# Self-attention with a hand-written step order: one transpose, two loads and one ScalarE pair change their places

## The reference

```
h = _layernorm(x, ln1_g, ln1_b)
x = x + _mha(h, h, sa_wq, sa_bq, sa_wk, sa_bk, sa_wv, sa_bv, sa_wo, sa_bo)
...
scores = jnp.einsum('bhqd,bhkd->bhqk', q, k) * HD ** (-0.5)     # 16 heads of 32 channels
p = jax.nn.softmax(scores, axis=-1)
o = jnp.einsum('bhqk,bhkd->bhqd', p, v)
return o @ wo.T + bo
```

## Time and profile before

| | us |
|---|---|
| median of 3 runs (3400.57 to 3406.2) | 3404.1 |
| the profiled execution | 3406.2 |
| its span | 3404.4 |
| PE busy in it | 3162.3 (93%) |
| DVE, ACT, POOL busy | 1820.2 (53%), 1574.4 (46%), 1327.8 (39%) |
| mean granted clock of PE | 0.964 |

### The profile page before, as it was taken

One profiled execution on the slowest core, in us unless ns is written; L12 is line 12 of the kernel. 1 busy time (PEld: TensorE's weight loads), 2 busy tenths in 40 slices (PEclk: granted clock), 3 DMA queues, 4 the chain that ended last, 5 costly groups with the idle time before them and its releaser, 6 DMA issues. The chain is left out here.

```text
span 3404.4 us, 41927 instructions
## 1 busy us (share of the span) xinstructions
PE 3162.3 (93%) x14480; PEld 2509.9 (74%) x14480; DVE 1820.2 (53%) x2848; ACT 1574.4 (46%) x2980; POOL 1327.8 (39%) x1355
## 2 busy tenths in 40 slices
PE   6599997999999976999999999849999799999999
PEld 5478876888888864677777777537787588888887
DVE  4588863333223224888788888758887432222221
ACT  2366653322222213777777777716666232222222
POOL 0344541333333331766666666734554111111110
PEclk8799998999999997999999999979999899999999
DMA  3423313211111114344444434332231321111000
GB/s 132 124 57 89 87 54 115 84 50 50 44 47 47 41 44 121 105 123 108 109 124 122 115 97 110 95 103 60 82 84 54 114 78 38 38 38 38 32 28 27
DMA packets 215045, 264.33 MB, mean 78 GB/s; under 512 B 78459, under 2 KB 100579, under 8 KB 214835
## 3 DMA queue, kind: packets, MB, share of 16 engines
q1 hardware_dynamic: 214835, 261.66, 26.0%
HBM read 125.12 MB, written 60.42 MB: 55 GB/s over the span
## 5 line engine op out<-in xcount | busy, mean ns | idle before, releaser
L1101 DVE TENSOR_REDUCE L1sa_nmax<-L1sa_s 128x2 f32<-128x1024 f32 x256 | 310.5, 1213 | 135.1 <-PE L1sa_s L907 134.2
L1206 POOL TENSOR_TENSOR L1sa_El<-L1sa_E,L1sa_Eh 128x1024 fp32r<-128x1024 f32 x128 | 314.0, 2453 | 129.2 <-ACT L1sa_Eh L1000 124.5
L468 DVE TENSOR_TENSOR L1ff_gl<-L1ff_gf,L1ff_gh 128x512 fp32r<-128x512 f32 x128 | 94.4, 738 | 474.7 <-ACT L1ff_gh L428 474.7
L468 DVE TENSOR_TENSOR L0ff_gl<-L0ff_gf,L0ff_gh 128x512 fp32r<-128x512 f32 x128 | 98.4, 769 | 437.9 <-ACT L0ff_gh L428 437.9
L414 ACT ACTIVATE L1ff_gf<-L1ff_f,cols 128x512 f32<-128x512 f32 x128 | 88.3, 690 | 450.3 <-PE L1ff_f L94 450.3
L414 ACT ACTIVATE L0ff_gf<-L0ff_f,cols 128x512 f32<-128x512 f32 x128 | 88.3, 690 | 449.8 <-PE L0ff_f L94 449.8
L1009 ACT ACTIVATE L1sa_E<-L1sa_st 128x1024 f32<-128x1024 f32 x256 | 258.9, 1011 | 8.6 <-PE L1sa_st L919 8.6
L92 PE MATMUL L1ff_f<-L1ff_hTh,L1ff_Wh 128*128 128x512 f32 x512 | 203.1, 397 | 5.7 <-POOL L1ff_hTl L235 5.7
L92 PE MATMUL L0ff_f<-L0ff_hTh,L0ff_Wh 128*128 128x512 f32 x512 | 202.9, 396 | 5.7 <-POOL L0ff_hTl L235 5.7
L1000 ACT ACTIVATE L1sa_Eh<-L1sa_E 128x1024 fp32r<-128x1024 f32 x192 | 200.6, 1045 | 0.2
L93 PE MATMUL L1ff_f<-L1ff_hTh,L1ff_Wl 128*128 128x512 f32 x512 | 200.3, 391 | 0.0
(11 more groups left out here) (282 smaller groups left out, 8531.4 us busy)
## 6 DMA issues: line engine op xcount, KB each, us to landing
L1sa_OLN<-L1sa_osb SPq DMA_DIRECT2D x128, 192.0 KB, 2.7
L0ff_xs<-x SPq DMA_DIRECT2D x64, 256.0 KB, 2.9
L1sa_stack_q<-L1sa_parts_q SPq DMA_DIRECT2D x128, 128.0 KB, 2.6
L1sa_stack_k<-L1sa_parts_k SPq DMA_DIRECT2D x128, 128.0 KB, 2.6
L1ff_xs<-x SPq DMA_DIRECT2D x64, 256.0 KB, 3.5
L0ca_xs<-in_x SPq DMA_DIRECT2D x32, 256.0 KB, 3.1
L0ca_stage<-in_x SPq DMA_DIRECT2D x32, 256.0 KB, 2.8
x<-L0ca_stage SPq DMA_DIRECT2D x32, 256.0 KB, 2.0
```

The source lines that it names most:

```text
L468: nc.vector.tensor_tensor(gl[:, j % 2, :], gf[:, j % 2, :], f32(gh[:, j % 2, :]), ALU.subtract)\
L1101: nc.vector.reduce_max(nmax[:, h % 2, 2 * (n % 2):2 * (n % 2) + 2], s_bank[:, :, :], AX.X, negate=True)\
L1206: nc.gpsimd.tensor_tensor(El[:, n % 2, :], E[:, n % 3, :], f32(Eh[:, n % 2, :]), ALU.subtract)\
```

## The change

Three edits, all in the order of the self-attention stage.

1. `SA_T_HALVES`: tile 1 of the next image is transposed in half 26 (step 13), not in half 24 (step 12).
2. On SP the load of tile 3 of the next image moves from step 13 to step 14, and the load of tile 1 of the image after that from step 16 to step 17.
3. On ACT the pair `o_hi` of a group comes ahead of the `e_hi` of its step, not behind it.

```diff
-SA_T_HALVES = (22, 24, 28, 30)
+SA_T_HALVES = (22, 26, 28, 30)
...
-                    if s in (12, 13) and b + 1 < B:
-                        load(b + 1, 2 + (12, 13).index(s))
-                    if s in (15, 16) and b + 2 < B:
-                        load(b + 2, (15, 16).index(s))
+                    if s in (12, 14) and b + 1 < B:
+                        load(b + 1, 2 + (s - 12) // 2)
+                    if s in (15, 17) and b + 2 < B:
+                        load(b + 2, (s - 15) // 2)
...
                 for n in steps_of(b):
+                    for g in range(GROUPS):
+                        if n == 8 * g + (17 if g % G == 0 else 11):
+                            o_hi(g)
                     if n % 2 == 0 and n >= 2:
                         o_out((n - 2) // 2)
                     if 0 <= n + 1 < PAIRS and EH_BY[(n + 1) % 8] == "act":
                         e_hi(n + 1)
-                    for g in range(GROUPS):
-                        if n == 8 * g + (17 if g % G == 0 else 11):
-                            o_hi(g)
```

## The result

| | before | after |
|---|---|---|
| median (lowest to highest), us | 3405.2 (3400.6 to 3407.7) | 3467.4 (3462.5 to 3471.1) |
| ratio to before, 95% interval | | 1.0183 [1.0166, 1.0202] |
| profiled execution, us | 3406.2 | 3465.9 |
| its span, us | 3404.4 | 3464.1 |

The change makes the kernel 62 us slower; 41 were forecast.

A forecast was written before the change was run, and what follows sets the result against it. The prediction took PE to set the pace in self-attention and summed 27.6 (load) + 10.7 (clock) - 5 (given back) + 0 (edit 1) + 8 (edit 3) = 41.3 us, forecasting 3446 us; the 8-in-10 range was 3422 to 3468.

The forecast's parts named there:

- The load behind the eight stack DMAs: PE stalls before transposing tile 3: 3.77 us in six images, 5.0 in the first, 27.6 us in all.
- The clock: Behind each tile 3 stall PE's clock falls to 0.50 for 3.4 us, costing 1.5 us; seven times, 10.7 us.
- rival (b): Behind each tile 3 stall 6.8 us at clock 0.50, nothing given back: +57 us, 3461; chance 0.20.
- Rival (a): Behind the tile 3 stalls the clock holds and o_hi costs nothing: +23 us, 3427; chance 0.19.
- Edit 1: Transpose of tile 1 moved from step 12 to 13 only changes steps on PE: 0 us, between -1 and +3.
- What the stall gives back: Other engines catch up during the stall, shortening PE's step 18 wait: 0.8 us in each of six images, -5 us.
- Edit 3: o_hi ahead of e_hi idles ACT in steps 19 and 27, delaying exp and PE: 1.0 us per image, +8 us.
- DVE's queue holds it: Step 4: the low part, for which PE waits 0.46 us, is held by DVE's queue; an earlier o_hi doesn't help.
- rival (c): Stack DMAs leave SP soon enough for tile 3's load to land in time; relief remains: -9.5 us, 3395; chance 0.05.

## Why the prediction was right in its sign and short in its size

- **The load behind the eight stack DMAs: right.** 3.63 to 3.75 us in each of six images against 3.77 forecast, and 4.5 in the first against 5.0, 26.7 us in the seven; a tile ahead of the first another 1.4 us stand, 0.6 before. The whole row grew by 28.1 us against 27.6. The reading of the slot from the residual load held to 0.01 us on SP. The run with the load ahead of the eight DMAs shows that this queue is the cause.
- **The clock: right in its sum, not in its reason.** A fall came each time. In four images it was the short one of 3.4 us and cost 1.4 us, forecast 1.5. In three, the first, the second and the fifth, it was as long as rival (b) had it, 6.8 us, but began within the stall, so that it cost 2.1 to 2.4 us and not 3.1. All seven make 12.4 us, by the times from tile 3's transpose to the end of the wait in step 19 against those of the run with PE kept at work (13.64 us in the first image, 14.12 in the last four); 10.7 were forecast. Rival (a), that the clock holds, did not come here. But the reason, that a stall of 3.8 us is long enough "so I expect the fall each time", is not what the runs show: with edit 2 alone and with L105 of group 0 late, one stall of seven (3.69 and 3.71 us) had no fall behind it, and three falls in the run with PE kept at work stood behind waits of 0.95 to 1.86 us. Seven of seven was in part luck.
- **Edit 1: right**, nothing.
- **What the stall gives back, -5: failed.** The step "starts its next maximum only at 1518.46, which today comes just in time; so I count 0.8 us" saw that DVE's row of work is the next limit and still took a gain from in front of it. L929's waits did fall, by 6.0 us; L907's rose by 9.4. With edit 2 alone the one replaces the other (1.11 for 1.10). With edit 3 as well L105 is held longer there, and it is 1.73. DVE, then PE, in the fourth image of the changed kernel:

```profile
1765.32 1.22 DVE L1101 TENSOR_REDUCE L1sa_nmax<-L1sa_s 128x2 f32<-128x1024 f32 x1 [1.57 <-PE L1sa_s L907]
1766.46 2.29 DVE L105 TENSOR_TENSOR L1sa_oTl<-L1sa_onorm,L1sa_oTh 128x512 fp32r<-128x512 f32 x1
1768.68 3.35 DVE L1115 RECIPROCAL L1sa_OLN<-L1sa_OLN 128x256 f32<-128x256 f32 x2
1771.95 1.15 DVE L1101 TENSOR_REDUCE L1sa_nmax<-L1sa_s 128x2 f32<-128x1024 f32 x1
```

```profile
1773.16 0.73 PE L907 MATMUL L1sa_s<-L1sa_stack_k,L1sa_stack_q 96*128 96x512 f32 x2 [1.73 <-DVE L1sa_nmax L1101]
```

- **Edit 3, +8: mis-sized.** It measured +19. The two delays that the prediction followed along ACT came at 0.66 and 0.47 us, near the 1.0 us per image it took. Missing was step 4: a third delay of 0.37 us at its start, which the wait for L105 behind it was to hide, and would have, had L105 not come later itself; that wait is 0.92 instead of 0.46. "DVE's queue holds it" was wrong: POOL's L1206 holds it, and this edit moves L1206. The waits for the exponential and for L105 make (16.1 - 3.1) + (16.8 - 14.0) = 15.8 us of the 19; beside them L929's waits rise by 3.1, from 9.8 to 12.9, and L907's fall by 2.1.
- **The sum.** The waits of the whole stage, 45.1, and the clock's 12.4 make 57.5 of the 59.7 us between the spans; the other 2.2 have no name. The forecast had 41.3; the relief that turned into a loss is 8.4 us of the difference (-5 against +9.4 - 6.0) and edit 3 some 11, of which a part is the same L105. (In rival (c) the 2.3 us for the eight DMAs should be 1506.09 - 2.97 - 1501.02 = 2.1; nothing hangs on it.)

The number fell inside the range, by 0.6 us, because rival (b) had opened it upwards, for another reason: that was luck.

## What to carry to other kernels

A DMA that is moved behind a batch in an in-order queue is late by the batch, and the slot can be read to hundredths of a microsecond from whatever stands there today. A wait that goes is worth only the distance to the next limit; look for the next instruction that the same engines owe, before counting a gain. A fall of the clock seen behind one stall isn't certain behind the next of the same length; put a chance on it and a price, not a rule. Where a VectorE instruction runs longer than another of its shape, lay GpSimd's timeline beside it before taking the duration as its own: a change of order on a third engine can stretch it, and moving it is only worth something where GpSimd isn't reading.

## What the runs showed of the hardware that was not expected

- VectorE's subtraction of two SBUF tiles waits for a GpSimd instruction that is under way and then does its whole work: it ends 0.54 to 0.56 us behind it with 512 columns (0.68 alone) and 1.08 to 1.09 with 1024 (1.22 alone), behind a GpSimd instruction on two tiles. It also works the other way: in the kernel before, a POOL L1206 that began at 1514.67, within an L105 (until 1515.26), took 2.84 us instead of 2.40; all 16 L1206 of that kernel over 2.5 us began within an L105 or an L1109. The maxima, which read one input, from PSUM, never took more than 1.23 us in the kernel before, whatever POOL did.
- One issue of a stack DMA on SP took 1.72 us where its neighbours took 0.60. With PE kept at work there are 11 such issues over 1 us; seven of the other traces have one or two (the changed kernel one of 1.36 at 1982.40, edit 2 alone one of 1.89 at 1967.04), and four have none, the kernel before among them. The cause is open.
- TensorE's clock went to 0.50 for 3.4 us behind waits of PE of 0.9 to 1.9 us, and stayed at 1.00 behind two stalls of 3.7 us.
